# A later unit for the router's logits, and a row of scales in the softmax's buffer

## The chip, the cores and the metric

The kernel runs on one core of one Trainium2 chip. Its time is the device time of one execution in microseconds (us). The engines are TensorE (PE), VectorE (DVE), ScalarE (ACT), GpSimd (POOL), and SyncE (SP), which here only issues transfers.

## What is computed

Two gated residual blocks over x of 16 batches, 1024 tokens, width 512. First cross attention to 64 memory tokens per batch (4 query heads, one key/value head of 128), then a mixture of experts in which, for each group of 32 tokens, each of 128 expert slots takes the token with the highest logit.

```python
x = x + tanh(g_xattn) * xattn(layernorm(x), ctx, mask, ...)     # rmsnorm, q, k, rope, softmax over 64, values, out_w
x = x + tanh(g_ffn) * ffn(layernorm(x), Wc, bc, W1, b1, W2, b2)
# ffn, per group of 32 tokens:
logits = einsum('bntd,des->bntes', grouped, Wc) + bc + tie
perm = (logits == max(logits, over the 32 tokens))
inner = relu(einsum(perm-gathered tokens, W1) + b1)
out = scatter(einsum(inner, W2) + b2, perm)
```

The router's logits are taken of layernorm(x1), x1 being the output of the first block. The kernel gets them as a product of Wc with x and another with the attention's values, and multiplies every token's column by the token's scale r = 1/sqrt(var + eps).

## The kernel before, in words

There are two stages, each written as five streams, one per engine, that meet only in semaphores. The order within a stream is written out by hand.

**Attention** (`attention`) runs over 32 units u of 512 tokens (`NU`, half a batch each) in a software pipeline: pass g of every engine's loop handles the softmax and values of unit g, the queries of unit g+1, and the splitting of x for unit g+2. TensorE's pass (`tensor`): transposes of the logits (L906), three of four query products of the next unit (L879), `part_of_x` of the next unit (L939), transposes of the softmax's result `pr` (`probs_T`, L913), the fourth query product, `part_of_values` (L952), the attention's values (L926) with the attention's logits between them (L894).

**The router's logits** pass through the ring `lx` of `LX_RING` places. ScalarE copies the part from x there (`part_of_x`, L595), VectorE adds the part from the values (`both_parts`, L726), GpSimd multiplies by the row of scales `rrow` (`scaled_logits`, L535), and SP stores the result to `lg_scratch` (L355). ScalarE's copy of unit u waits until the store of unit u - LX_RING has landed. In ScalarE's stream the copies `probs` (pTh, L589) stand behind it; VectorE's pTl (L705) follows them, and part_of_values needs both.

**The row of scales.** GpSimd's `row_scale(u)` (L505 to L511) makes r of unit u at the end of pass u+1. SP's `logits_out(u)` stores it to `r_scratch` (L351), waits until it landed, loads it back broadcast to 128 partitions as `rrow` (L353), waits for the product, and stores the logits (L355). SP calls it for unit u-1 within its turn for unit u, between the store of the unit's second half of x1 (L427) and the reload of that place with x of unit u+4 (L433). GpSimd takes the product of unit g-2 in pass g right behind the softmax's two products `pr` (L543), and then come the rotation (L528, L529), the split `xTl` (L515), `norm_scale` and `row_scale`.

**Between the stages.** SP ends the stage with `logits_out` of unit 31, waits for the last stores, and loads W1's second ring piece, which lies in the last quarter of `xin` (L458).

**Experts** (`experts`) runs over the 16 batches: gather (L1380) and first layer (L1407) in eight pieces of W1, the scatter of the batch before (L1446), second layer (L1431), routing of the next batch. W1's pieces 2, 4 and 5 are resident; piece 3, the middle piece, is loaded to `xin` (`load_middle`, L1185), the four end pieces run through a ring of two (`load_end`, L1177). GpSimd scales the tokens of the next batch in place (`Router.normed`, L182; tiles 0 to 3 early, 4 to 7 late) and issues the accumulating stores of the batch before (`add_to_out`, L1236), the last four of them once the last moved piece of W2 has landed. The first gather of the second half needs tile 7. The middle piece's quarters wait for the last four of those stores.

Of the kernel before, what the change touches and what calls it, by code (L numbers as in the profile page):

```python
# [17 lines left out]
P = 128  # L18
# [6 lines left out]
NT = T // P  # L25
# [13 lines left out]
LX_RING = 3  # L39
# [29 lines left out]
def build(nc, x, xT_in, ctx_in, ctxT_in, mask, gx_in, gf_in, rms, q_w, kv_w, out_w, out_wT, Wc, bc, W1, b1, W2, b2,  # L69
# [7 lines left out]
    with top:  # L77
# [29 lines left out]
        attn = attention(nc, top, ps, ident, small, gate_x, gate_f, xin, xT, consts, const_loads, kept, kept_loads, d_kept,  # L107
                         ring, ring_loads, d_ring, route, m_b2s, x, xT_in, ctx_in, ctxT_in, mask, gx_in, gf_in, rms, q_w, kv_w, out_w, out_wT, Wc,
                         ident_in, cos_in, sin_in, b2, kr_dram, vc_dram, out)
        ffn = experts(nc, top, ps, kept, d_kept, consts, ident, gate_f, xin, ring, d_ring, route, m_b2s, W1, W2, out)  # L110
# [105 lines left out]
def attention(nc, top, ps, ident, small, gate_x, gate_f, xin, xT, consts, const_loads, kept, kept_loads, d_kept,  # L216
# [17 lines left out]
    with st:  # L234
# [19 lines left out]
        rrow = sb("rrow", [P, HT])  # L254
# [50 lines left out]
        mean_of = qs[:, 0, 0:P]  # L305
        gts = sb("gts", [P, 2])
# [38 lines left out]

        def sync(e):
            def logits_out(u):

                i, h = u // 2, u % 2
                e.wait_ge(route.m_r.sem, route.m_r.at(i, h))  # L350
                e.dma_start(route.r_dram[i, h], route.r[:, i, h * TH:(h + 1) * TH]).then_inc(d_r.sem, 16)  # L351
                e.wait_ge(d_r.sem, d_r.at(u))
                e.dma_start(rrow[:], route.r_dram[i, h].rearrange("p t -> (p t)").partition_broadcast(P)).then_inc(d_rr.sem, 16)  # L353
                e.wait_ge(m_lsr.sem, m_lsr.at(u))
                e.dma_start(route.lg_dram[i, h], lx[:, u % LX_RING, :]).then_inc(d_lgs[u % LX_RING].sem, 16)  # L355

# [52 lines left out]
            for u in range(NU):  # L409
# [7 lines left out]
                if u == NU - 1:  # L417
                    for n in range(2):
                        e.wait_ge(d_lgs[n].sem, d_lgs[n].at((NU - 3 - n) // LX_RING))
                    e.wait_ge(m_L.sem, m_L.at(NU - 1))  # L420
                    for h in range(2):
                        route.load_logits(e, 0, h)
                k = u % RING
                for h in range(2):
                    v = slice(2 * h, 2 * h + 2)
                    e.wait_ge(m_rs.sem, m_rs.at(u, 2 * h + 1))
                    e.dma_start(unit_tokens(x1_dram, u)[:, v], xin[:, k, v]).then_inc(d_o[k].sem, 16)  # L427
                    if h and u:
                        logits_out(u - 1)
                    if u + RING < NU:  # L430
                        e.wait_ge(d_o[k].sem, d_o[k].at(u // RING, h))
                        e.wait_ge(m_s1.sem, m_s1.at(u, 2 * h + 1))
                        e.dma_start(xin[:, k, v], unit_tokens(x, u + RING)[:, v]).then_inc(d_x[k][h].sem, 16)  # L433
                    if h == 0 and unit(u + 3):
                        e.wait_ge(m_lo.sem, m_lo.at(u + 2, C - 1))
                        e.dma_start(xT[:], turned_x(u + 3)).then_inc(d_xT.sem, 16)
# [15 lines left out]
            logits_out(NU - 1)  # L452
            for k in (2, 3):
                e.wait_ge(d_o[k].sem, d_o[k].at(NU // RING - 1, 1))
            for k in range(LX_RING):
                e.wait_ge(d_lgs[k].sem, d_lgs[k].at((NU - 1 - k) // LX_RING))
            for c in range(QUARTERS):
                e.dma_start(quarter(ring[1], c), quarter(ring_loads[1], c)).then_inc(d_ring[1][c].sem, 16)  # L458

        def gpsimd(e):  # L460
# [70 lines left out]
            def scaled_logits(u):  # L531
                o = lx[:, u % LX_RING, :].rearrange("p (t s) -> p t s", s=P)
                e.wait_ge(m_ls.sem, m_ls.at(u))
                e.wait_ge(d_rr.sem, d_rr.at(u))
                e.tensor_tensor(o, o, rrow[:].rearrange("p (s t) -> p t s", t=TH), ALU.mult).then_inc(m_lsr.sem, 1)  # L535

            for g in range(-1, NU):
                if unit(g):
                    for tp in range(2):
                        e.wait_ge(m_rc.sem, m_rc.at(g, tp))  # L540
                        if g:
                            e.wait_ge(m_PT.sem, m_PT.at(g - 1, tp))
                        e.tensor_tensor(heads(pr_[:, tp, :]), heads(lg[:, tp, :]),  # L543
                                        rc[:, tp, :].unsqueeze(2).broadcast_to([P, 8, S]), ALU.mult).then_inc(m_pr.sem, 1)
                if unit(g - 2):
                    scaled_logits(g - 2)
# [16 lines left out]
                if unit(g - 1):  # L563
                    row_scale(g - 1)
                if g >= NU - 2:
# [479 lines left out]
        return Stage(sync, gpsimd, scalar, vector, tensor)  # L1045


def experts(nc, top, ps, kept, d_kept, consts, ident, gate_f, xin, ring, d_ring, route, m_b2s, w1_dram, w2_dram, out):
# [7 lines left out]
    with st:  # L1056
# [114 lines left out]
        def sync(e):  # L1171
# [33 lines left out]
            for i in range(B + 1):  # L1205
                if live(i):
                    if i != 1:
                        for c in range(QUARTERS):
                            load_middle(i, c)
                    for k, c in ((0, 0), (0, 1), (1, 0), (1, 1), (1, 2), (1, 3), (0, 2), (0, 3)):  # L1210
# [21 lines left out]
        def gpsimd(e):  # L1232
# [5 lines left out]
            for i in range(B):  # L1238
# [3 lines left out]
                for t in range(NT):  # L1242
                    if live(i - 1):
                        if t == NY:
                            e.wait_ge(d_room[W2_MOVED[2]].sem, d_room[W2_MOVED[2]].at(i, QUARTERS - 1))
                        add_to_out(i - 1, t)
                if live(i + 1):
                    for t in range(NY, NT):
                        route.normed(e, i + 1, t)
# [283 lines left out]
```

## Time and profile before

| what | value |
|---|---|
| median of 3 runs | 1894.57 us (1873.33 to 1895.8) |
| profiled execution | 1886.3 us, span 1884.5 us |
| TensorE busy | 1668.2 us, 89% |
| VectorE busy | 1292.8 us, 69% |
| GpSimd busy | 854.0 us, 45% |
| ScalarE busy | 724.3 us, 38% |
| mean granted clock of TensorE | 0.959 of full |

The span is from the first to the last instruction, and the profiled execution's own time is 1.8 us longer. Busy time is counted per engine and says nothing on what it waits for; for that there are the list of waits, the chain of waits (the work that ended last, followed back from release to release) and the timeline. The attention stage lasts to about 1000 us of the span.

### The profile page before, as it was taken

Reading aid. Unit: us, or ns where it says so; the run is one execution under the profiler, and the core shown is the slowest. Engines: PE = TensorE matmul, PEld = TensorE weight load, DVE = VectorE, ACT = ScalarE, POOL = GpSimd, SP = SyncE. Lnnn points to the kernel's source line nnn. Section 1 sums busy time; section 2 is a strip of 40 time slices with the busy share of each in tenths; the row PEclk is TensorE's granted clock in tenths of the full one; section 3 lists DMA queues with packets and bytes.
Section 4 is the critical chain, followed back from the end, with each engine's and each line's share of the span. In section 5 each row is a group of like instructions: output and inputs, shape, how many; then the busy total and the mean of one; then the engine's idle time right before and its main releaser. Section 6 shows DMA issues by size and latency. Waiting matters only on the chain.

```text
span 1884.5 us, 51838 instructions
## 1 busy us (share of the span) xinstructions
PE 1668.2 (89%) x22488; PEld 1167.2 (62%) x22488; DVE 1292.8 (69%) x1886; ACT 724.3 (38%) x965; POOL 854.0 (45%) x1016
## 2 busy tenths in 40 slices
PE   7898989889889889898985799989998999999895
PEld 4676667667667666676764455666665555556662
DVE  6676766766767666676663477777777777777676
ACT  3532222322222222222211455555555555555452
POOL 3466666766766766667661122212222222221212
PEclk9999999999999999999987899999999999999998
DMA  7524434435444354344443488777777888887676
GB/s 264 159 102 147 161 116 135 166 111 178 137 134 140 114 168 138 128 140 132 150 145 112 153 220 220 218 205 220 206 208 213 216 225 225 218 216 210 190 187 165
DMA packets 180882, 324.81 MB, mean 172 GB/s; under 512 B 23344, under 2 KB 33328, under 8 KB 179248
## 3 DMA queue, kind: packets, MB, share of 16 engines
q1 hardware_dynamic: 135728, 239.68, 38.7%
q0 software_dynamic: 17280, 31.46, 10.0%
q10 hardware_dynamic: 27648, 50.34, 8.3%
q8 instruction: 179, 2.93, 0.7%
q14 instruction: 47, 0.39, 0.1%
HBM read 242.71 MB, written 78.71 MB: 171 GB/s over the span
## 4 chain that ended last, share of the span: by engine, by line
POOL 32%; PE 29%; DMA 23%; issue 9%; DVE 3%; ACT 2%; ACTq 1%; SPq 1%; POOLq 0%; DVEq 0%
PE ps L1407 13%; POOL xTl L515 8%; DMA gat<-in_W 8%; PE ps L1380 7%; DMA r_scratch<-r_all 7%; DMA rrow<-r_scratch 6%; POOL qc L528 4%; POOL qc L529 4%; POOL xin L182 3%; POOL lx L535 3%; POOL vw L552 2%; POOL r_all L507 2%; PE ps L1431 2%; POOL r L489 2%; POOL r L497 2%
## 5 line engine op out<-in xcount | busy, mean ns | idle before, releaser
L182 POOL TENSOR_SCALAR xin<-xin,r_all,nb_all 128x512 f32<-128x512 f32 x128 | 115.3, 1178 | 400.5 <-DMA xin<-out 400.4
L1312 DVE STREAM_TRANSPOSE res<-res 128x2048 f32<-128x2048 f32 x128 | 292.1, 2295 | 0.1
L1264 ACT ACTIVATE gat<-ps 128x1536 f32<-128x1536 f32 (+1 forms) x128 | 171.3, 1344 | 249.1 <-PE ps L1380 249.1
L879 PE MATMUL ps<-xTh,qh 128*128 128x512 f32 x512 | 209.3, 409 | 5.3 <-DVE qs L694 1.4
L1328 DVE COPY res<-ps 128x1024 f32<-128x1024 f32 x128 | 156.7, 1225 | 82.3 <-PE ps L1431 82.3
L1236 POOL DMA_DIRECT2D out<-xin x120 | 105.9, 1166 | 232.7 <-DMA gat<-in_W 151.6
L1380 PE MATMUL ps<-sel,xin 32*128 32x128 f32 x4096 | 161.5, 294 | 52.0 <-POOL xin L182 27.4
L879 PE MATMUL ps<-xTh,ql 128*128 128x512 f32 x512 | 200.3, 391 | 0.0
L879 PE MATMUL ps<-xTl,qh 128*128 128x512 f32 x512 | 199.9, 390 | 0.0
L1318 DVE COPY gat<-ps 128x512 f32<-128x512 f32 (+1 forms) x128 | 103.9, 813 | 118.6 <-PE ps L1380 117.6
L926 PE MATMUL ps<-vw,pTh 128*128 128x512 f32 x512 | 180.2, 436 | 0.0
L1380 PEld LDWEIGHTS ps<-sel,xin 32*128 32x128 f32 x4096 | 137.9, 197 | 66.4 <-issue 41.9
L1274 ACT ACTIVATE res<-ps 128x1024 f32<-128x1024 f32 x128 | 131.1, 1024 | 92.7 <-PE ps L1431 92.7
L515 POOL TENSOR_TENSOR xTl<-xT,xTh 128x512 fp32r<-128x512 f32 x128 | 160.4, 1283 | 12.3 <-ACT xTh L578 12.3
L595 ACT ACTIVATE lx<-ps 128x512 f32<-128x512 f32 x32 | 19.1, 597 | 348.1 <-DMA lg_scratch<-lx 323.4
L709 DVE TENSOR_TENSOR xin<-ps,xin 128x512 f32<-128x512 f32 x128 | 88.2, 689 | 88.1 <-PE ps L926 88.1
L926 PEld LDWEIGHTS ps<-vw,pTh 128*128 128x128 f32 x512 | 106.1, 212 | 49.6 <-issue 25.2
L528 POOL TENSOR_TENSOR qc<-qc,qs 128x512 f32<-128x512 f32 x64 | 82.4, 1287 | 113.8 <-DVE qs L694 113.8
L705 DVE TENSOR_TENSOR pTl<-ps,pTh 128x512 fp32r<-128x512 f32 x64 | 41.3, 686 | 134.4 <-ACT pTh L589 134.4
L535 POOL TENSOR_TENSOR lx<-lx,rrow 128x512 f32<-128x512 f32 x32 | 49.3, 1540 | 180.7 <-DMA rrow<-r_scratch 180.7
L1407 PE MATMUL ps<-gat,xin 128*64 128x64 f32 x3072 | 102.7, 225 | 18.3 <-DMA xin<-in_W 17.1
L879 PEld LDWEIGHTS ps<-xTh,qh 128*128 128x128 f32 x512 | 96.2, 188 | 36.0 <-DVE qs L694 18.8
(156 smaller groups left out, 3399.2 us busy)
## 6 DMA issues: line engine op xcount, KB each, us to landing
gat<-in_W ACTq DMA_DIRECT2D x192, 256.0 KB, 5.6
xT<-in_xT SPq DMA_DIRECT2D x32, 1024.0 KB, 6.6
xin<-in_x SPq DMA_DIRECT2D x64, 512.0 KB, 3.8
out<-xin SPq DMA_DIRECT2D x64, 512.0 KB, 2.9
xin<-out SPq DMA_DIRECT2D x128, 256.0 KB, 4.4
xin<-in_W SPq DMA_DIRECT2D x128, 256.0 KB, 3.6
out<-xin POOLq DMA_DIRECT2D x120, 256.0 KB, 8.6
xT<-in_W SPq DMA_DIRECT2D x68, 256.0 KB, 4.4
```

Of the source, the lines that this page charges most:

```text
L182: e.tensor_scalar(self.xn[:, t, :], self.xn[:, t, :], self.r[:, i, t:t + 1], self.nb[:, i, t:t + 1], ALU.mult, ALU.add).then_inc(self.m_xn ...
L515: e.tensor_tensor(xTl[:, c, :], xT[:, c, :], xTh[:, c, :].bitcast(F32), ALU.subtract).then_inc(m_lo.sem, 1)
L528: e.tensor_tensor(qc[:, 2 * p, :], qc[:, 2 * p, :], qs[:, 2 * p + 1, :], ALU.subtract).then_inc(m_rot.sem, 1)
L879: last = e.matmul(ps[:, 2 + n % 2, :], a[:, c, n * DH:(n + 1) * DH], b[:, c, :], start=(k == 0), stop=(k == len(parts) - 1))
L926: last = e.matmul(ps[:, 5 + t % 2, :], a[:, t // 2, column:column + P], vw[:, u // 2 % 2, k, p, :], start=(m == 0), stop=(m == len(parts) ...
L1236: e.dma_start(batch(out, b, t, 1)[:, 0], tile_of(t), accum_op=ALU.add).then_inc(d_ys[t].sem, 16)
L1264: e.activation(o, v, ACT.Copy).then_inc(m_gaA.sem, 1)
L1274: e.activation(o, v, ACT.Copy).then_inc(m_evA.sem, 1)
L1312: e.transpose(v, v).then_inc(m_tr.sem, 1)
L1328: e.tensor_copy(o, v).then_inc(m_evV.sem, 1)
L1380: last = e.matmul(ps[:, front(n) + g, t * E:(t + 1) * E], xn[r, h * TH + t, c * P:(c + 1) * P], sel[r, h * TH + t, :], start=True, stop=True)
L1407: last = e.matmul(ps[a * 64:(a + 1) * 64, q // 8, q % 8 * 64:(q % 8 + 1) * 64], first(i, p)[:, (e0 % 64) * F:(e0 % 64 + 2) * F], gat[:, c ...
```

## The change

The ring `lx` gets a fourth place, and the whole path of a unit's logits behind the row of scales comes a unit later on SP: in its turn for unit u SP stores and reloads the scales of unit u-2 (`scales_back`, ahead of the unit's stores, behind a wait for the unit's transposes of the softmax) and stores the logits of unit u-2 (`logits_out`). `rrow` is no longer a buffer of its own but the first half of `pr_`. GpSimd takes the product at the end of its pass. The logits of unit 31 go out from the experts' stream, behind the loads of W1's middle piece (`last_logits`); W1's second ring piece is loaded behind `scales_back` of unit 30. In the experts, GpSimd's four later norms alternate with the four later stores, a norm first.

```diff
-LX_RING = 3
+LX_RING = 4
...
-        rrow = sb("rrow", [P, HT])
...
+        rrow = pr_[:, 0, :]
...
+        def scales_back(e, u, g):
+
+            i, h = u // 2, u % 2
+            e.wait_ge(route.m_r.sem, route.m_r.at(i, h))
+            e.dma_start(route.r_dram[i, h], route.r[:, i, h * TH:(h + 1) * TH]).then_inc(d_r.sem, 16)
+            e.wait_ge(d_r.sem, d_r.at(u))
+            e.wait_ge(m_PT.sem, m_PT.at(g, 1))
+            e.dma_start(rrow, route.r_dram[i, h].rearrange("p t -> (p t)").partition_broadcast(P)).then_inc(d_rr.sem, 16)
+
+        def logits_out(e, u):
+            e.wait_ge(m_lsr.sem, m_lsr.at(u))
+            e.dma_start(route.lg_dram[u // 2, u % 2], lx[:, u % LX_RING, :]).then_inc(d_lgs[u % LX_RING].sem, 16)
+
+        def last_logits(e):
+
+            scales_back(e, NU - 1, NU - 1)
+            logits_out(e, NU - 1)
+            for k in range(LX_RING):
+                e.wait_ge(d_lgs[k].sem, d_lgs[k].at((NU - 1 - k) // LX_RING))
+
         def sync(e):
-            def logits_out(u):
...
                 if u == NU - 1:
                     for n in range(2):
-                        e.wait_ge(d_lgs[n].sem, d_lgs[n].at((NU - 3 - n) // LX_RING))
+                        e.wait_ge(d_lgs[n].sem, d_lgs[n].at((NU - 4 - n) // LX_RING))
...
+                if u >= 2:
+                    scales_back(e, u - 2, u)
...
-                    if h and u:
-                        logits_out(u - 1)
+                    if h and u >= 2:
+                        logits_out(e, u - 2)
...
-            logits_out(NU - 1)
             for k in (2, 3):
                 e.wait_ge(d_o[k].sem, d_o[k].at(NU // RING - 1, 1))
-            for k in range(LX_RING):
-                e.wait_ge(d_lgs[k].sem, d_lgs[k].at((NU - 1 - k) // LX_RING))
+            scales_back(e, NU - 2, NU - 1)
+            e.wait_ge(m_s1.sem, m_s1.at(NU - 1, TH - 1))
             for c in range(QUARTERS):
                 e.dma_start(quarter(ring[1], c), quarter(ring_loads[1], c)).then_inc(d_ring[1][c].sem, 16)
+            logits_out(e, NU - 2)
...
                         if g:
                             e.wait_ge(m_PT.sem, m_PT.at(g - 1, tp))
+                        if g >= 3 and tp == 0:
+                            e.wait_ge(m_lsr.sem, m_lsr.at(g - 3))
...
-                if unit(g - 2):
-                    scaled_logits(g - 2)
                 if unit(g + 1):
                     rotated(g + 1, 0)
...
                 if unit(g - 1):
                     row_scale(g - 1)
+                if unit(g - 2):
+                    scaled_logits(g - 2)
...
                     if i != 1:
                         for c in range(QUARTERS):
                             load_middle(i, c)
+                    if i == 0:
+                        last_logits(e)
...
-                for t in range(NT):
+                if live(i - 1):
+                    for t in range(NY):
+                        add_to_out(i - 1, t)
+                    e.wait_ge(d_room[W2_MOVED[2]].sem, d_room[W2_MOVED[2]].at(i, QUARTERS - 1))
+                for t in range(NY, NT):
+                    if live(i + 1):
+                        route.normed(e, i + 1, t)
                     if live(i - 1):
-                        if t == NY:
-                            e.wait_ge(d_room[W2_MOVED[2]].sem, d_room[W2_MOVED[2]].at(i, QUARTERS - 1))
                         add_to_out(i - 1, t)
-                if live(i + 1):
-                    for t in range(NY, NT):
-                        route.normed(e, i + 1, t)
```

## Rows read from the trace of the kernel before

**Rows 1.** Page of the profile, part 4: the chain that ended last, by line.

```profile
PE ps L1407 13%; POOL xTl L515 8%; DMA gat<-in_W 8%; PE ps L1380 7%; DMA r_scratch<-r_all 7%; DMA rrow<-r_scratch 6%; POOL qc L528 4%; POOL qc L529 4%; POOL xin L182 3%; POOL lx L535 3%; POOL vw L552 2%; POOL r_all L507 2%; PE ps L1431 2%; POOL r L489 2%; POOL r L497 2%
```

**Rows 2.** Chain in order of time, one unit: start us, us, what.

```profile
517.61 3.40 DMA r_scratch<-r_all
...
521.02 3.15 DMA rrow<-r_scratch
...
524.31 1.54 POOL lx L535
```

**Rows 3.** Waits, 120 to 960 us: who for whom: us in total, times, longest.

```profile
ACT lx L595 <- DMA lg_scratch<-lx: 312.5, 28, 13.4
...
POOL lx L535 <- DMA rrow<-r_scratch: 152.6, 29, 6.7
...
PE ps L952 <- DVE pTl L705: 74.8, 27, 4.4
```

**Rows 4.** Timeline: start us, us, engine, line, operation [idle before <-releaser].

```profile
528.26 0.60 ACT L595 ACTIVATE lx<-ps 128x512 f32<-128x512 f32 x1 [10.51 <-DMA lg_scratch<-lx]
...
530.92 0.47 PE L952 MATMUL ps<-pTh,voh 128*128 128x512 f32 x1 [2.48 <-DVE pTl L705]
```

**Rows 5.** Timeline of TensorE: transposes of the softmax in four of the units.

```profile
127.71 1.03 PE L913 MATMUL ps<-ident,pr 128*128 128x128 f32 x8
...
152.73 1.03 PE L913 MATMUL ps<-ident,pr 128*128 128x128 f32 x8
...
933.54 1.03 PE L913 MATMUL ps<-ident,pr 128*128 128x128 f32 x8
...
958.89 1.03 PE L913 MATMUL ps<-ident,pr 128*128 128x128 f32 x8
```

**Rows 6.** Windows: stretch, us, busy (x) PE PEld DVE ACT POOL, PEclk, DMA, GB/s.

```profile
400.00:700.00 300.00, 272.97 (x1281) 205.35 (x1280) 203.35 (x432) 76.32 (x135) 202.03 (x242) 0.97 0.44 145
...
532.50:536.80 4.30, 4.30 (x13) 3.13 (x11) 1.39 (x2) 0.42 (x1) 4.27 (x4) 0.61 0.00 0
...
933.54:958.89 25.35, 25.09 (x124) 18.83 (x122) 18.72 (x40) 7.09 (x13) 19.44 (x24) 1.00 0.32 104
```

**Rows 7.** Timeline of GpSimd in the unit of 933.54 to 958.89 us.

```profile
952.35 0.20 POOL L511 TENSOR_TENSOR nb_all<-mv,ns 128x4 f32<-128x4 f32 x1
952.50 2.05 POOL L543 TENSOR_TENSOR pr<-lg,rc 128x512 f32<-128x512 f32 x2
```

**Rows 8.** DMA issues, 120 to 960 us: times, KB each, median us to landing.

```profile
rrow<-r_scratch SPq DMA_DIRECT2D x29, 256.0 KB, 3.2
lg_scratch<-lx SPq DMA_DIRECT2D x29, 256.0 KB, 2.2
...
r_scratch<-r_all SPq DMA_DIRECT2D x29, 2.0 KB, 4.3
```

**Rows 9.** Waits of SP's queue, 120 to 960 us.

```profile
SPq L427 <- DVE xin L709: 301.1, 58, 11.0
```

**Rows 10.** Chain in order of time, from attention to experts.

```profile
1001.54 4.55 DMA r_scratch<-r_all
1006.11 4.43 DMA rrow<-r_scratch
...
1023.28 3.22 DMA xin<-in_W
```

**Rows 11.** Timeline of TensorE there: first layer's second product, seventh product.

```profile
1026.55 3.69 PE L1407 MATMUL ps<-gat,xin 128*64 128x64 f32 x64 [17.11 <-DMA xin<-in_W]
...
1044.30 1.97 PE L1407 MATMUL ps<-gat,xin 128*64 128x64 f32 x62
```

**Rows 12.** Waits, 1080 to 1800 us.

```profile
PE ps L1380 <- POOL xin L182: 26.1, 15, 4.4
```

**Rows 13.** Timeline of GpSimd in one batch: later stores, then later norms.

```profile
1380.71 3.54 POOL L1236 DMA_DIRECT2D out<-xin  x4 [11.75 <-DMA gat<-in_W]
1382.92 4.33 POOL L182 TENSOR_SCALAR xin<-xin,r_all,nb_all 128x512 f32<-128x512 f32 x4
```

More of the change, by code:

```diff
@@ L106, in build @@
         ring_loads = [W1[0], W1[1]]
-        attn = attention(nc, top, ps, ident, small, gate_x, gate_f, xin, xT, consts, const_loads, kept, kept_loads, d_kept,
+        attn, last_logits = attention(nc, top, ps, ident, small, gate_x, gate_f, xin, xT, consts, const_loads, kept, kept_loads, d_kept,
                          ring, ring_loads, d_ring, route, m_b2s, x, xT_in, ctx_in, ctxT_in, mask, gx_in, gf_in, rms, q_w, kv_w, out_w, out_wT, Wc,
                          ident_in, cos_in, sin_in, b2, kr_dram, vc_dram, out)
-        ffn = experts(nc, top, ps, kept, d_kept, consts, ident, gate_f, xin, ring, d_ring, route, m_b2s, W1, W2, out)
+        ffn = experts(nc, top, ps, kept, d_kept, consts, ident, gate_f, xin, ring, d_ring, route, m_b2s, last_logits, W1, W2, out)
         with nc.Block() as blk:
@@ L344, in attention @@
         turned_x = lambda u: xT_in[u // 2].rearrange("(c p) t -> p c t", p=P)[:, :, u % 2 * HT:(u % 2 + 1) * HT]
-        def sync(e):
-            def logits_out(u):
[L349 to L355, printed above, removed]
+        def scales_back(e, u, g):
[13 more added lines that the diff above has]
+                e.wait_ge(d_lgs[k].sem, d_lgs[k].at((NU - 1 - k) // LX_RING))
+        def sync(e):
             e.dma_start(rs1[:], rms).then_inc(d_rs.sem, 16)
@@ L534, in scaled_logits @@
                 e.wait_ge(d_rr.sem, d_rr.at(u))
-                e.tensor_tensor(o, o, rrow[:].rearrange("p (s t) -> p t s", t=TH), ALU.mult).then_inc(m_lsr.sem, 1)
+                e.tensor_tensor(o, o, rrow.rearrange("p (s t) -> p t s", t=TH), ALU.mult).then_inc(m_lsr.sem, 1)
             for g in range(-1, NU):
@@ L1043, in tensor, with experts @@
             e.wait_ge(m_rs.sem, m_rs.at(NU - 1, TH - 1))
-        return Stage(sync, gpsimd, scalar, vector, tensor)
-def experts(nc, top, ps, kept, d_kept, consts, ident, gate_f, xin, ring, d_ring, route, m_b2s, w1_dram, w2_dram, out):
+        return Stage(sync, gpsimd, scalar, vector, tensor), last_logits
+def experts(nc, top, ps, kept, d_kept, consts, ident, gate_f, xin, ring, d_ring, route, m_b2s, last_logits, w1_dram, w2_dram, out):
     st = ExitStack()
```

## The prediction

> **What bounds the kernel now.** I read the chain of waits by line first. Besides TensorE's product lines it holds three steps that compute nothing: the store of r_scratch, the load of rrow from it, and GpSimd's idle time before the product with it [rows 1]. The chain in order of time shows them one after the other in a unit of the attention stage: 3.40 us for the store, 3.15 us for the load, then the product of 1.54 us [rows 2]. The list of waits of 120 to 960 us says who pays. ScalarE's copy of a unit's x part (part_of_x) waits 28 times, 312.5 us in all, for a store of logits, because the ring lx has three places; GpSimd waits 152.6 us in 29 units for rrow. TensorE itself waits 74.8 us in 27 units, always before part_of_values, for pTl [rows 3]. The timeline links them: the copy starts 10.51 us late, the pTh copies stand behind it on ScalarE, pTl behind these, and TensorE idles 2.48 us [rows 4].
>
> What a unit would take without this is in the trace. From one unit's first transpose of the softmax to the next it was 25.02 us while the ring was still filling, and 25.35 us once late in the stage, where no idle time stood before part_of_values. Between them, 152.73 to 933.54 us, lie 27 units, and with the last one 28: (958.89 - 152.73)/28 = 28.79 us each [rows 5]. The idle time is not the whole of the difference. Behind the gap the clock falls to one of its two levels: 0.61 granted over 4.3 us, so mostly 1.2 GHz, against 1.00 in the undisturbed unit [rows 6].
>
> **The change part by part, attention.** (1) LX_RING 4: part_of_x(g+1) waits for the store of unit g-3, no longer g-2. (2) The product with rrow moves from behind the softmax's products to the end of GpSimd's pass. In the undisturbed unit GpSimd ended row_scale at 952.35 + 0.20 = 952.55 us and the two softmax products, 2.05 us, followed at once [rows 7]. With 1.54 us put ahead of them they end at 956.1 us; TensorE wants them at 958.89 us [rows 5]. Slack 2.8 us, so the move costs nothing; without that slack each us late costs one per unit. (3) The logits' store is issued at 952.55 + 1.54 = 954.1 us and lands in 2.2 us [rows 8], at 956.3 us, 2.6 us before the next x part is ready to be copied. (4) rrow now lies in the softmax's own buffer and must wait for its transposes, which in that unit end at about 933.54 + 1.03 = 934.6 us [rows 5]. SP, which has done the previous unit's second reload by then, needs 4.3 + 3.2 us for store and load [rows 8]: rrow is there by 942 us, needed at 952.6 us, slack 10 us. Added waits: one of SP on the transposes, one of GpSimd on its own last product (free, that engine runs in order). Behind SP's wait are the unit's two stores, its reload of x and that of xT. They wait for the second attention sum anyway: SP stands idle for these sums 301.1 us in 58 stores, 5 us each [rows 9], and that idle time covers what is put ahead. No instruction or byte is added; eight wait instructions or so move.
>
> So TensorE becomes the bound of the stage. I take 25.2 us a unit, between the two undisturbed ones: 28 x (28.79 - 25.2) = 100.5 us. The unit behind 958.89 us has a small gap and slow clock too, and gives about 3 us. Bounds: 28 x (28.79 - 25.35) = 96 us and 28 x (28.79 - 25.02) = 106 us. **Attention: -103 us.**
>
> Against this stands a reading by busy share. TensorE was busy 272.97 of 300 us in mid stage [rows 6]: 27 us idle in 10.4 units, 2.6 us each, or 28 x 2.6 = 73 us. The Trainium skill (Perfetto Trace Analysis, Identifying the Most-Contended Engine) says matmul busy time is no good measure of distance from the limit; the trace agrees, as matmuls at 1.2 GHz count as busy. By busy share the whole sum would be -90 us, by the undisturbed units it is the one below.
>
> **Transition.** TensorE stands 17.11 us before the second product with W1's ring piece, up to 1026.55 us [rows 10, 11]. SP issues that piece only at 1023.28 us, behind both detours of unit 31: store, rrow, product, store of logits [rows 10]. After the change only the last stores' landing (to about 1006 us, as the 4.55 us row), one r_scratch store and the issue of rrow lie ahead: issue at about 1008 us, landed like before with 3.22 us plus the rrow load in front of it, 1012 us. Gain 14.5 us. Part is given back. The middle piece follows unit 30's logits (1012 + 1.5 us) in two rounds of 3.2 us and some issue, lands by 1021 us, in time for its product at about 1020 us. Then SP does unit 31's detour from 1018 us: 4.3 + 3.2 + 1.5 + 2.2 us, to about 1029.5 us, and only then loads W1's two end pieces. Their products begin 17.75 us behind the second [rows 11], so at 1029.8 us; their quarters land from 1033.5 to 1038 us. That costs 6.5 us. **Transition: -8 us**; bounds -14 (nothing given back) and -2.
>
> SP's detour is priced by its rows. [...] The 4.3 us row of a 2 KB store speaks for queueing behind other traffic, so I keep the rows.
>
> **Experts.** GpSimd today issues four adds and then scales tiles 4 to 7: 3.54 us of issue and norms to 1387.25 us from 1380.71 us [rows 13], so 0.88 us per add and about 0.8 us per norm. TensorE waits for the last norm 26.1 us in 15 batches [rows 12]. With one norm ahead of each add, the last norm has three adds before it instead of four: up to 0.88 us earlier, where GpSimd and not the load of the tile is late. The last add comes later by up to 3 us; behind it is the reload of W1's middle piece, which is needed far later, and on SP the ring pieces. I take -0.4 us x 14 = **-6 us**; bounds -12 (0.88 in every batch) and +8 (half a us lost in each through SP's queue).
>
> Sum: -103 - 8 - 6 = -117 us on the profiled execution's 1886.3 us: 1769 us. The median is 8 us above that execution. What varies between runs are mostly transfers on the chain, and the new unit has slack against them; I take 1771 us.
>
> **Rivals.** A: the ring's wait stays in part. The store may land later than 2.2 us, or SP be late for it. The slack is 2.6 us and another us or so behind it before TensorE feels it; stores that land 2 us beyond that would cost 1.5 us per unit with the slow clock, 42 us: 1813 us. For it: the r_scratch row of 4.3 us for 2 KB. Against: the logits' own row. Chance 0.11. B, **slower**: rrow is late, now that its load hangs on the transposes and on SP's queue, and the softmax's products stand behind the product with it. It decides from 942 + 10 + 2.8 = about 955 us on, 13 us later than forecast; each us more costs 28. To be over 2% slower than now a unit must take 30.2 us, so rrow must come 5 us later still: 1935 us. Against: the same two transfers end 7 us after their start today. Chance 0.02. C: the pacing engine is another, GpSimd with its chain from the rotation through xTl and norms to the products; then the ring's gain is lost and the time stays near 1885 us. For it: GpSimd leads the chain's lines [rows 1]. Against: it sat idle for rrow 5 us a unit [rows 3]. Chance 0.04.
>
> **Numbers.** My forecast holds 0.83: its own range is 1748 to 1800 us (bounds of the three terms, and some 10 us between runs). To leave out no more than 2 in 10, I go to 1808 us for the mild part of A. A measurement tells 2% from no change: under 1857 us is faster. A and the forecast lie there, with 0.01 of A beyond: 0.93. C: 0.05 with that. B: 0.02.
>
> **What would show it.** Right: ScalarE's wait on the logits' store nearly gone, units of 25.0 to 25.4 us, clock 1.00 in the stage, TensorE's gap before part_of_values gone; one gap of 2 to 4 us at W1's second piece and a new one at its end pieces; the last add of a batch 3 us later. Wrong: softmax's transposes waiting for their products (B, C), or the ring's wait over 4 us a unit (A). The forecast fails if an engine other than TensorE ends the unit.

## The result, and the profile after

| | before | after |
|---|---|---|
| median, us | 1886.67 (1873.33 to 1895.8, 4 runs) | 1772.31 (1766.51 to 1775.78, 4 runs) |
| profiled execution, its span | 1886.3, 1884.5 | 1775.6, 1773.8 |
| mean granted clock | 0.959 | 0.977 |

Ratio 0.940, interval [0.932, 0.947]: 6% faster. The forecast was 1771 us. The time between two marks on TensorE's timeline splits the profiled pair. A unit is the time from the first transpose of the softmax in the 3rd unit to that in the 31st, over 28. The tail goes from there to the experts' first gather, the transition from there to batch 1's first gather, the experts from there to the first product of the last batch's scatter.

| stretch, us | before | after | change | forecast |
|---|---|---|---|---|
| 28 units | 28 x 28.79 | 28 x 24.99 | -106.6 | -100.5 |
| tail | 42.3 | 38.6 | -3.7 | -3 |
| transition | 73.1 | 68.9 | -4.2 | -8 |
| experts | 784.7 | 790.1 | +5.4 | -6 |

**Attention.** TensorE's transposes of the softmax in three units of the changed kernel, the 3rd, the 31st and the last, which answer to [rows 5] (columns as there):

```profile
151.01 1.03 PE L927 MATMUL ps<-ident,pr 128*128 128x128 f32 x8
...
850.60 1.03 PE L927 MATMUL ps<-ident,pr 128*128 128x128 f32 x8
871.63 2.12 PE L927 MATMUL ps<-ident,pr 128*128 128x128 f32 x8 [7.31 <-POOL pr L557]
```

The 28 units between the first two take 699.6 us, 24.99 us each. The list of waits, 120 to 850 us, answers to [rows 3]:

```profile
ACT lx L609 <- PE ps L953: 210.5, 28, 8.0
...
ACT lx L609 <- DMA lg_scratch<-lx: 8.6, 1, 8.6
...
POOL pr L557 <- POOL lx L547: 4.7, 28, 0.2
```

ScalarE now waits for TensorE's part_of_x and not for a store; one wait that the profile puts down to a store is left, and it is hardly longer than the waits for TensorE. No row with TensorE waiting for pTl is left. GpSimd does not wait for rrow in any of these units: no such row is in the list either. In mid stage the windows view (columns as [rows 6]) has 298.62 of 300 us busy, at clock 1.00:

```profile
400.00:700.00 300.00, 298.62 (x1467) 227.16 (x1466) 233.36 (x494) 93.82 (x156) 236.16 (x277) 1.00 0.51 162
```

GpSimd's timeline in a unit, which answers to [rows 7]:

```profile
544.39 1.55 POOL L547 TENSOR_TENSOR lx<-lx,pr 128x512 f32<-128x512 f32 x1
...
546.11 2.05 POOL L557 TENSOR_TENSOR pr<-lg,rc 128x512 f32<-128x512 f32 x2 [0.17 <-POOL lx L547]
```

Its softmax products end at 548.16 us and TensorE's transposes of them begin at 550.77 us, 2.6 us later; in the next unit it was 3.3 us. The forecast had 2.8 us.

The last unit shows what the moved product costs when rrow is late. TensorE stands 7.31 us before the transposes above at 871.63 us. In the kernel before it stood 4.51 us at the same place, when VectorE's part of the softmax was late there:

```profile
980.79 2.17 PE L913 MATMUL ps<-ident,pr 128*128 128x128 f32 x8 [4.51 <-POOL pr L543]
```

So the late rrow costs 2.8 us of the 7.31. The chain of waits there is

```profile
855.15 7.12 DMA r_scratch<-r_all
862.29 3.61 DMA pr<-r_scratch
```

SP issues the 2 KB store at 855.15 us, right behind nine loads for the next stage. The store takes 7.12 us beside them, rrow lands at 865.9 us, and the product and four norms (L182) stand ahead of the last softmax products. This is rival B, in one unit of 32.

**Transition.** TensorE's timeline, which answers to [rows 11]:

```profile
899.33 0.69 PE L1424 MATMUL ps<-gat,xin 128*64 128x64 f32 x16 [1.86 <-DMA xin<-in_W]
900.65 2.83 PE L1424 MATMUL ps<-gat,xin 128*64 128x64 f32 x48 [0.64 <-DMA xin<-in_W]
...
910.65 0.69 PE L1424 MATMUL ps<-gat,xin 128*64 128x64 f32 x16 [1.23 <-DMA xin<-in_W]
...
925.20 2.03 PE L1424 MATMUL ps<-gat,xin 128*64 128x64 f32 x32 [7.63 <-DMA xin<-in_W]
928.11 1.12 PE L1424 MATMUL ps<-gat,xin 128*64 128x64 f32 x16 [0.88 <-DMA xin<-in_W]
929.79 1.12 PE L1424 MATMUL ps<-gat,xin 128*64 128x64 f32 x16 [0.56 <-DMA xin<-in_W]
```

The 17.11 us are 2.50 us now, and a new idle time of 9.07 us stands at the end pieces. SP's timeline says why. The first end piece's loads are issued behind the store of unit 31's logits:

```profile
893.79 1.86 SPq L469 DMA_DIRECT2D xin<-in_W  x4
...
906.99 0.43 SPq L350 DMA_DIRECT2D r_scratch<-r_all  x1
...
915.51 0.32 SPq L357 DMA_DIRECT2D lg_scratch<-lx  x1
...
917.65 1.01 SPq L1191 DMA_DIRECT2D xT<-in_W  x2
```

**Experts.** Waits, 970 to 1690 us, which answer to [rows 12], and behind them, for the kernel before, two more rows of the view of [rows 12], 1080 to 1800 us:

```profile
PE ps L1397 <- issue: 17.2, 18, 1.7
...
PE ps L1424 <- issue: 11.7, 12, 3.0
...
PE ps L1397 <- POOL xin L182: 6.4, 11, 1.0
```

```profile
PE ps L1380 <- issue: 12.7, 12, 1.5
...
PE ps L1407 <- issue: 2.5, 4, 1.4
```

The wait for the norm fell from 26.1 to 6.4 us, and idle time of these two lines that the profile puts down to no wait ("issue") rose from 15.2 to 28.9 us. The experiments ask what that is, and whether the experts really lost 5 us.

### The profile page after: what moved, and what is told of

Same layout as the page of the kernel before. It is cut to its first block, busy times and chain, and to the rows that moved or that the text cites. A ratio compares the mean times of both kernels' runs of the same rounds, so it can differ in the third digit from the quotient of the medians.

```text
span 1773.8 us, 51856 instructions
## 1 busy us (share of the span) xinstructions
PE 1639.1 (92%) x22488; PEld 1152.8 (65%) x22488; DVE 1295.8 (73%) x1886; ACT 737.3 (42%) x965; POOL 856.1 (48%) x1016
## 4 chain that ended last, share of the span: by engine, by line
PE 60%; DMA 16%; DVE 11%; issue 5%; ACT 3%; POOL 2%; SPq 1%; ACTq 1%; POOLq 0%; DVEq 0%
PE ps L1424 13%; PE ps L893 10%; PE ps L940 10%; PE ps L1397 7%; PE ps L953 5%; DMA xin<-out 4%; DMA out<-xin 4%; DMA gat<-in_W 3%; PE ps L908 3%; PE ps L1448 3%; PE ps L966 3%; DVE mx L691 2%; PE ps L1463 2%; PE ps L927 2%; ACT lg L660 2%
## 5 line engine op out<-in xcount | busy, mean ns | idle before, releaser
L182 POOL TENSOR_SCALAR xin<-xin,r_all,nb_all 128x512 f32<-128x512 f32 x128 | 114.3, 897 | 533.0 <-DMA xin<-out 387.1
L1397 PEld LDWEIGHTS ps<-sel,xin 32*128 32x128 f32 x4096 | 133.9, 188 | 57.0 <-issue 30.1
L1252 POOL DMA_DIRECT2D out<-xin x120 | 121.4, 1086 | 94.6 <-DVE xin L1168 81.1
L940 PE MATMUL ps<-vw,pTh 128*128 128x512 f32 x512 | 164.6, 402 | 0.0
L707 DVE TENSOR_TENSOR qc<-ps,cos 128x512 f32<-128x512 f32 x128 | 86.8, 678 | 58.6 <-PE ps L893 58.3
L1424 PE MATMUL ps<-gat,xin 128*64 128x64 f32 x3072 | 108.0, 231 | 17.4 <-DMA xin<-in_W 12.8
L940 PEld LDWEIGHTS ps<-vw,pTh 128*128 128x128 f32 x512 | 94.3, 189 | 45.5 <-issue 25.2
L893 PEld LDWEIGHTS ps<-xTh,qh 128*128 128x128 f32 x512 | 96.2, 188 | 35.5 <-DVE qs L708 18.3
L1424 PEld LDWEIGHTS ps<-gat,xin 128*64 128x64 f32 x3072 | 101.0, 145 | 23.8 <-issue 14.2
```

Of the source, the lines that this page charges most:

```text
L182: e.tensor_scalar(self.xn[:, t, :], self.xn[:, t, :], self.r[:, i, t:t + 1], self.nb[:, i, t:t + 1], ALU.mult, ALU.add).then_inc(self.m_xn ...
L893: last = e.matmul(ps[:, 2 + n % 2, :], a[:, c, n * DH:(n + 1) * DH], b[:, c, :], start=(k == 0), stop=(k == len(parts) - 1))
L940: last = e.matmul(ps[:, 5 + t % 2, :], a[:, t // 2, column:column + P], vw[:, u // 2 % 2, k, p, :], start=(m == 0), stop=(m == len(parts) ...
L1252: e.dma_start(batch(out, b, t, 1)[:, 0], tile_of(t), accum_op=ALU.add).then_inc(d_ys[t].sem, 16)
L1397: last = e.matmul(ps[:, front(n) + g, t * E:(t + 1) * E], xn[r, h * TH + t, c * P:(c + 1) * P], sel[r, h * TH + t, :], start=True, stop=True)
L1424: last = e.matmul(ps[a * 64:(a + 1) * 64, q // 8, q % 8 * 64:(q % 8 + 1) * 64], first(i, p)[:, (e0 % 64) * F:(e0 % 64 + 2) * F], gat[:, c ...
```

## The experiments

All medians stand beside a run of the kernel before on the same chip (1873 to 1887 us). Stretches are cut as in the table above.

**1. Was it the ring, or the two transfers ahead of the logits' store?** The kernel before, ring of three, without store and reload of the scales.

```diff
             def logits_out(u):
-                e.wait_ge(route.m_r.sem, ...)
-                e.dma_start(route.r_dram[i, h], ...)
-                e.wait_ge(d_r.sem, d_r.at(u))
-                e.dma_start(rrow[:], ...)
                 e.wait_ge(m_lsr.sem, m_lsr.at(u))
...
+            e.memset(rrow[:], 1.0).then_inc(d_rr.sem, 16)
...
-                e.wait_ge(d_rr.sem, d_rr.at(u))
+                e.wait_ge(d_rr.sem, d_rr.at(0))
```

The product is made with a row of ones, so this kernel leaves the scales out of the router's logits.

> The kernel before, its ring of three places and its order kept, with only the detour of the scales left out: no store to r_scratch, no load of rrow; the product is made with a row of ones, so the router's logits go out unscaled. Theory 1 (the two transfers hold the product back, hence the logits' store, hence ScalarE's copy and TensorE): softmax transposes 25.0 us apart at clock 1.00 with three places already, ScalarE's wait on lg_scratch under 20 us in all, and with the transition's detours gone too about 1760 us. Rival (three places are too few for this order whatever the transfers do): units stay above 27 us and ScalarE goes on waiting several us per unit for lg_scratch, time above 1830 us.

Measured: 1771.39 us (1767.76 to 1775.01), ratio 0.944 [0.936, 0.952]; unit 24.995 us. The waits of 120 to 850 us:

```profile
ACT lx L592 <- PE ps L936: 218.7, 29, 8.1
```

No wait on a store is in the list. So three places are enough where SP does not hold the logits back for the detour: the ring was too small only for the 6.5 us of [rows 2]. A fourth place with the path a unit later, and three places with the shorter path, buy the same unit, and both stop at it: TensorE is the bound at 25.0 us. A fourth place alone, with the detour and the product where they were, was not run, so its share is not shown. Both kernels also free GpSimd of its wait for rrow. That this wait cost TensorE nothing by itself is read from the list before, where TensorE never waits for the softmax's products from 120 to 960 us; no run tests it alone. The later product with a ring of three wasn't tried: at the end of pass g it would free the place that ScalarE wants within pass g.

**2. How much slack has GpSimd ahead of the transposes?** Idle operations of 1 us in each pass of 2 to 29, behind the product: two, then five.

```diff
                     scaled_logits(g - 2)
+                if 2 <= g < NU - 2:
+                    for k in range(2):      # 5 in the second kernel
+                        e.tensor_tensor(idle[:, k, :], eps_l[:, 0:TH], nhalf[:, 0:TH], ALU.pow)
```

> The changed kernel with two idle pow instructions of 1.02 us each at the end of GpSimd's passes 2 to 29, ahead of the softmax's products. Theory (GpSimd has 2.6 to 3.3 us of slack before the transposes): no change, within 4 us of 1772 us, units still 25.0 us, transposes not waiting. Rival (GpSimd's chain is as long as TensorE's and only looks hidden): each us shows, 28 x 2 = 56 us more.

> The changed kernel with five idle pow instructions of 1.02 us each at the same place, 5.1 us in a pass. Theory (slack 2.6 to 3.3 us): the excess of 1.8 to 2.5 us shows in every one of 28 units, 60 us, with slow clock behind the gap up to 100 us: 1830 to 1870 us, TensorE waiting for the softmax's product in every unit. Rival (GpSimd has far more slack, nothing there could have turned into a bound): under 1790 us.

Measured: with two 1769.80 us (1761.95 to 1777.66), unit 24.996 us, no change. With five 1804.86 us (1804.61 to 1805.12), unit 26.39 us, less than expected. GpSimd's and then TensorE's timeline with five:

```profile
568.71 4.92 POOL L582 TENSOR_TENSOR idle<-eps_layer,nhalf 128x4 f32<-128x4 f32 x5
```

```profile
574.70 0.66 PE L931 MATMUL ps<-ident,pr 128*128 128x128 f32 x4 [0.95 <-POOL pr L558]
575.70 0.65 PE L931 MATMUL ps<-ident,pr 128*128 128x128 f32 x4 [0.34 <-POOL pr L558]
```

The transposes come in two groups of four, and the first needs only the first of the two softmax products, which ends 1.02 us before the second. So the slack is about 2.6 + 1.0 = 3.6 us, and 4.92 - 3.6 = 1.3 us is about what a unit grew by (26.39 - 24.99 = 1.4). The two waits of a unit make 1.0 us of that on average (25.3 us in 26 units); the rest is counted as busy time. An extra loss through the clock, as in [rows 6], didn't come: TensorE's 52 waits for the softmax are of 1.0 us at most, and the windows view grants 1.00.

```profile
PE ps L931 <- POOL pr L558: 25.3, 52, 1.0
```

```profile
400.00:700.00 300.00, 287.58 (x1386) 214.46 (x1386) 222.93 (x471) 91.71 (x148) 277.29 (x323) 1.00 0.48 158
```

**3. Is the new end of the attention worth anything?** The changed kernel with the old order there.

```diff
             scales_back(e, NU - 2, NU - 1)
-            e.wait_ge(m_s1.sem, m_s1.at(NU - 1, TH - 1))
+            logits_out(e, NU - 2)
+            last_logits(e)
             ... # W1's second ring piece
-            logits_out(e, NU - 2)
... # in the experts, behind the loads of W1's middle piece
-                    if i == 0:
-                        last_logits(e)
```

> The changed kernel with the end of the attention stage in the old order: unit 30's and unit 31's detours and logits first, then W1's second ring piece; no detour behind the middle piece. Theory (the transition as changed wins 15 us at the second product and gives 11 to 13 back at the end pieces, 4 us net): 3 to 6 us slower than the changed kernel, about 1777 us; TensorE waits some 17 us for the ring piece and nothing for the end pieces. Rival (my forecast of 8 us net): 8 us or more slower.

Measured: 1773.96 us (1772.69 to 1775.98), transition 71.66 us against 68.91. Its waits, 860 to 960 us, have one long wait, and none at the end pieces:

```profile
PE ps L1422 <- DMA xin<-in_W: 16.1, 1, 16.1
```

Moving that wait to the end pieces saves 2.75 us in the trace. The medians, 1.6 to 4 us apart, can't confirm it.

**4. The experts' GpSimd order.** The changed kernel with four later stores first, then four norms, as before.

```diff
+                for t in range(NT):
+                    if live(i - 1):
+                        if t == NY:
+                            e.wait_ge(d_room[W2_MOVED[2]].sem, ...)
+                        add_to_out(i - 1, t)
+                if live(i + 1):
+                    for t in range(NY, NT):
+                        route.normed(e, i + 1, t)
```

> The changed kernel with the experts' order of before on GpSimd: four later stores, then four later norms. Theory F (the norms no longer hold TensorE up, but the time is taken again by idle time marked issue, which the old wait had hidden): the same time as the changed kernel within 4 us, waits for the last norm back at 20 to 26 us, issue idle lower by about the same. Rival (the alternation is worth the 18 us that the wait list shows): 1785 to 1790 us. Second rival (the alternation costs time through the later reload of the middle piece): 5 us or more faster than the changed kernel.

Measured: 1783.05 us (1778.1 to 1791.6), experts 803.6 us in the profiled execution, which was the slowest of the six. The unaltered kernel had 1772.31 us, and 1769.97 us (1766.61 to 1783.81) in a later series: the old order costs 11 to 13 us. The kernel of experiment 3, which alternates and ran in the same series as this one, lies with all its six runs (1772.69 to 1775.98 us) below all six here. Waits, 970 to 1690 us:

```profile
PE ps L1396 <- POOL xin L182: 35.2, 14, 4.3
...
PE ps L1396 <- issue: 12.2, 14, 1.8
```

My theory, no net gain because issue idle takes over what the norm gives back, fell. Against 6.4 and 28.9 us in the changed kernel, 28.8 us of waits for the norm went, and 16.7 us of issue idle came: more than half is given back, not all. Over the whole of the experts the issue idle is 13 to 15 us in the three profiles with the old order and 22 to 33 us in the nine with the alternation. The kernel before and experiment 1 have the old order too, and their experts took 784.7 and 790.1 us. So the 11 to 13 us are shown for this kernel; what the order was worth in the kernel before is not.

**5. What is "issue"?** If the gaps sit at places of the instruction stream, eight more transposes ahead of the experts must move each gap by eight matmuls.

```diff
             e.wait_ge(m_pl.sem, m_pl.at(NU - 1, 1))
+            for k in range(8):
+                e.transpose(ps[:, 1, ...], route.selT[0][:, ...], ident[:])
             route.chosen_T(e, 0, 1)
```

> The changed kernel with eight transposes more (eight weight loads and eight matmuls, on a bank written anyway) just ahead of the last chosen_T between the stages. Theory F (the idle time marked issue lies where a block of TensorE's instruction stream ends): every such gap moves by eight matmuls, so that the groups behind it grow from x6, x9 and x39 to x14, x17 and x47, at unchanged cost. Rival (the gaps belong to operations, their operands or their waits): they stay before x6, x9 and x39. Time within 5 us of the changed kernel in both cases.

Measured: 1771.96 us (1771.59 to 1772.33). Three gaps of one batch on TensorE's timeline, in the changed kernel and in this one:

```profile
1127.07 0.50 PE L1397 MATMUL ps<-sel,xin 32*128 32x128 f32 x6 [1.06 <-issue]
...
1132.20 1.38 PE L1424 MATMUL ps<-gat,kept 128*64 128x64 f32 x39 [0.61 <-issue]
...
1142.06 0.59 PE L1397 MATMUL ps<-sel,xin 32*128 32x128 f32 x9 [1.36 <-issue]
```

```profile
1123.22 0.72 PE L1401 MATMUL ps<-sel,xin 32*128 32x128 f32 x14 [1.01 <-issue]
...
1128.13 1.62 PE L1428 MATMUL ps<-gat,kept 128*64 128x64 f32 x47 [0.40 <-issue]
...
1137.59 0.82 PE L1401 MATMUL ps<-sel,xin 32*128 32x128 f32 x17 [0.96 <-issue]
```

The groups left behind the gap grow from 6, 39 and 9 matmuls to 14, 47 and 17: eight each. It is so in the whole trace: counted in matmuls from the first gather, 30 of its 32 issue gaps lie exactly eight ahead of a place where one of the other thirteen traces has one. Those places are 126.3 matmuls apart, or a multiple of it, which with one weight load for each matmul makes 253 instructions. (One more gap, ahead of batch 0's second layer, stands at the same place in every trace and is not of this kind.) The gap belongs to a place in the stream and not to a step of the algorithm. The Trainium skill (Runtime: NRT & Kernel Launch, Instruction fetch mechanics) says that an engine's instruction memory is refilled in blocks of 256 instructions and that crossing a block is "mostly hidden". Gaps at fixed places of the stream, 253 instructions and some waits apart, agree with the blocks. "Mostly hidden" holds by count, as about 100 of the stage's 135 places show no gap; but the others cost 29 us in 30 gaps from 970 to 1690 us.

**6. Does the issue idle come from the data traffic?** The changed kernel with every weight load of the experts at a quarter of its columns, so that it computes with partly stale weights.

```diff
-                e.dma_start(quarter(ring[k], c), quarter(w1_dram[...], c))...
+                e.dma_start(quarter(ring[k], c)[:, 0:P], quarter(w1_dram[...], c)[:, 0:P])...
... # W1's middle piece and W2's moved ones in the same way
```

> The changed kernel with every load of expert weights in the experts' stage (moved pieces of W2, end pieces and middle piece of W1) cut to a quarter of its bytes, same number of transfers and instructions; the experts compute with partly stale weights. Theory F (TensorE's idle time marked issue, 29 us in the experts, always at nearly the same place of the instruction stream, is late instruction blocks behind the data traffic): issue idle in the experts falls to 10 us or less, time 1735 to 1750 us with the waits for weights gone. Rival (these gaps are fixed costs of the stream or lost records and have nothing to do with traffic): they stay at about 29 us and only the 10 us of waits for weights between the stages go, 1760 us or more.

Measured: 1694.98 us (1694.77 to 1695.18), 40 us below the range expected; experts 720.8 us, with no issue idle and no wait for a norm. The windows view of the experts, changed kernel first:

```profile
970.00:1690.00 720.00, 664.80 (x15589) 425.80 (x15584) 538.83 (x441) 391.19 (x442) 181.10 (x222) 0.99 0.79 213
```

```profile
970.00:1620.00 650.00, 628.51 (x15384) 403.00 (x15382) 529.18 (x436) 391.66 (x442) 184.26 (x224) 1.00 0.61 137
```

TensorE's busy share goes from 0.92 to 0.97 as the DMA engines' goes from 0.79 to 0.61. The gaps at the ends of instruction blocks are there only while the data transfers are dense. Of the 69 us that the stage is shorter by, 32 us are issue idle and 8 us waits for the norm. Another 31 us are busy time, 692 us against 723 us for the same products, and no run explains them.

The traces also hold the start and duration of every packet that the DMA engines moved, and these show the instructions themselves. In the experts of the changed kernel 135 packets of 16 KB pass the queue marked "instruction", as many as there are blocks of 126.3 matmuls. All 35 issue gaps of the stage end 1.25 to 1.61 us behind the landing of one of them, and of the 40 other gaps only one does; the landings are 5.7 us apart in the median. With the weight loads in full a packet starts 2.8 us (median) behind the end of the block before, with a quarter of them 0.7 us; once started it takes 1.0 and 1.1 us. So it is the start of the fetch that comes late beside dense data, not its transfer.

**7. Take back what the transition gives back.** First `last_logits` is split: the scales go behind the fourth of the end pieces' quarters, the store of logits ahead of the last. Then SP also issues the 2 KB store of the scales a turn earlier.

```diff
                     for k, c in (...):
+                        if i == 0 and (k, c) == (1, 2):
+                            last_logits[0](e)     # scales_back(31)
+                        if i == 0 and (k, c) == (0, 3):
+                            last_logits[1](e)     # logits_out(31)
                         load_end(i, k, c)
# second kernel, in SP's turn for unit u
                     if h and u >= 2:
                         logits_out(e, u - 2)
+                    if h and 1 <= u < NU - 1:
+                        scales_out(e, u - 1)      # no longer in scales_back
```

> The changed kernel with unit 31's detour spread between the loads of W1's end pieces: scales back after the fourth of the eight quarters, logits out before the last. Theory (the end pieces are late by the whole detour, 11 to 13 us): TensorE waits 3 us instead of 9 at the end pieces, 8 to 10 us faster than the changed kernel, about 1763 us. Rival (something else, as the loads of x for the next batch or the moved W2 pieces, comes late next): within 3 us of the changed kernel.

> The one before, and SP stores the scales of unit u-1 already in its turn u, behind the logits' store, so that turn u+1 only loads them. Theory (in unit 31 the softmax's product stands 2.9 us behind its reciprocal, as GpSimd waits 5.9 us for scales whose store took 7.1 us behind the kept and ring loads; elsewhere the detour has slack): 2 to 3 us faster than the split alone, units still 25.0 us. Rival (the load of the scales is late by the same traffic and nothing is won): within 1 us of it.

Measured: 1767.12 us (1762.9 to 1772.23), transition 62.63 us, less of a gain than expected; with the early store 1763.83 us (1756.46 to 1765.68), transition 62.23 us, tail 35.48 us against 38.05 with the split alone. Waits of the first, 860 to 960 us:

```profile
PE ps L1427 <- DMA xin<-in_W: 3.6, 2, 2.2
...
PE ps L1427 <- DMA xT<-in_W: 0.9, 1, 0.9
```

12.8 us of waits for W1 became 4.5. Is the sum of it in the time? The changed kernel and the one with the early store, both again, side by side:

> The changed kernel unaltered, in more rounds beside the others: about 1772 us. Its experts' part, 790 us in the first profile, should on this theory lie near 784 us on average (forecast -6 us against the old order, which gave 785 to 804 us), since e3 with the old order was 1783 us; rival: 790 us is its true size and the alternation brought nothing.

> The split with the early store of the scales again, beside the changed kernel in the same rounds: 8 to 10 us faster than that (6 us from the end pieces, 2.6 us from unit 31). Rival: under 4 us faster, the rest being spread between executions.

Measured: 1769.97 us (1766.61 to 1783.81), ratio 0.947 [0.943, 0.952], and 1766.34 us (1753.86 to 1779.66), ratio 0.944 [0.939, 0.949]. The stretches agree with the first runs (transition 64.5 against 68.2 us, tail 35.5 against 39.5 us), 7.7 us together, but the medians are 3.6 us apart, as the rival said, and the intervals overlap. It is the fastest kernel found, and that it beats the changed one is not shown.

**8. All four norms ahead of the later stores.** The kernel of 7 with the early store, to take the last 7 us of norm waits.

```diff
                 for t in range(NY, NT):
                     if live(i + 1):
                         route.normed(e, i + 1, t)
+                for t in range(NY, NT):
                     if live(i - 1):
                         add_to_out(i - 1, t)
```

> The one before with GpSimd's four later norms all ahead of the four later stores. Theory (the last norm has nothing ahead of it but norms, TensorE's wait of 7 us for it goes to 3 or less, but idle time marked issue takes most of it back): within 3 us of the one before. Rival 1 (norms are what is left to win): 5 us faster. Rival 2 (the stores, up to 3 us later, make the middle piece late): 5 us or more slower, with TensorE waiting for xin of W1 inside the batches.

Measured: 1788.15 us (1784.7 to 1792.85), 22 us slower, experts 806.9 us. Waits, 970 to 1690 us, of this kernel and then of the one it was made from:

```profile
DVE sel L191 <- DMA sel<-lg_scratch: 55.1, 11, 9.1
...
PE ps L1474 <- DVE xin L1176: 20.2, 8, 5.9
...
PE ps L1435 <- DMA xin<-in_W: 2.3, 2, 1.3
```

```profile
DVE sel L191 <- DMA sel<-lg_scratch: 14.4, 9, 6.3
...
PE ps L1473 <- DVE xin L1176: 2.5, 2, 2.3
```

My theory fell, and the second rival came by a way of its own. The wait for the norm is gone, and a dearer one took its place. W1's middle piece, for which SP waits on the later stores (85.0 us against 54.2 in its queue's list), costs TensorE only 2.3 us itself. But SP issues the load of the next logits behind it; VectorE waits 41 us more for them and finishes the outputs late, for which TensorE's scatter waits 18 us more. Alternating norm and store lies between two cliffs, 11 to 13 us on the one side and 22 us on the other.

## Why the prediction was right, and where a term was mis-sized

**Attention, right.** The chain as told was the cause: logits' store, part_of_x, pTh, pTl, part_of_values. Experiment 1 takes away only its head and gets all of the gain. The unit came out at 24.99 us, not the 25.2 that I took, at the lower undisturbed unit of [rows 5]: -106.6 us against -100.5, beyond the lower bound by less than 1 us. The reading by busy share, 73 us, fell. It missed 34 us, and most of that is the slow clock, which counts as busy: from 120 to 960 us the kernel before was granted 0.97, so about 25 us (an estimate) went there, in 16 stretches like the one of [rows 6], not one in every unit.

**The slacks, right in size, one read too strictly.** GpSimd 2.8 us forecast, 2.6 to 3.3 measured. But "without that slack each us late costs one" begins only at 3.6 us, as the first group of transposes needs one product alone (experiment 2). rrow was never late in the steady units, so the slack of 10 us was not used up. In unit 31, where the forecast looked only at SP's part, it came after 7.1 + 3.6 us of transfers and cost TensorE 2.8 us (7.31 against 4.51 before). The early store took 2.6 to 4.0 us of the tail away (experiment 7), which is that.

**Transition, gain right, give-back mis-sized.** From the first gather to the second product it took 10.16 us against 25.41 before: -15.25 us, forecast -14.5. Given back: second to seventh product 25.87 us against 17.75, +8.1; seventh product to the end of the eighth 9.1 against 3.9, +5.2; 13.3 in all where the term had 6.5; the rest of the stretch gave 2.3 more. The detour of unit 31 cost what I had priced it at, 10.7 us from 906.99 to 917.65 us against 11.2. What I priced too low are W1's quarters: I took the 3.22 us of [rows 10], which is the first and shortest of them. In the changed kernel those of the ring piece landed 5.5 to 6.7 us behind their issue, those of the middle piece 2.9 to 5.5 us and those of the end pieces 2.9 to 6.9 us. So the detour began 13.2 us behind the ring piece's issue and not 10, and the waits stand in the middle piece (1.23 us) and, in three, at the end pieces. -4.2 us lies within the bounds -14 and -2.

**Experts, the mechanism right, its size hidden in the pair.** "The last norm has three adds before it instead of four" is what happened: on GpSimd's timeline the last norm ends 5.8 us behind the wait ahead of it, in the batch from 1268.45 us, against 6.5 us in [rows 13]. But 26.1 us of waits became 6.4, where 6 of 26 was forecast. That is 1.3 us in each of 15 batches, more than the 0.88 us that I had as the most; where the rest comes from stays open. What failed is the silent premise that idle time taken from one wait stays away: 14 us of it came back as issue idle. The +5.4 us of the profiled pair is no measure of the change. Nine profiles with the alternating order have 777 to 790 us (mean 784), three with the old order 785 to 804 (mean 793), and by the medians of experiment 4 the order is worth 11 to 13 us, at the bound of -12.

The table's sum, -109 us, with 1.6 us outside its stretches, is the difference of the two profiled executions, 110.7 us. The forecast had 117: the terms' errors, -7 for attention with its tail, +4 and +11, cancel in part. That the median is so near the 1771 us has a share of luck, as it lies 3 us below its profiled execution.

The rivals: A (the ring's wait stays) did not come: one wait of 8.6 us in the stage. C (another engine paces) did not: five idle operations on GpSimd were needed to bring it about. B came in the last unit alone. Its price was summed wrongly: a unit of 30.2 us, or rrow 5 us later still, gives 1771 + 28 x 5 = 1911 us, 1% slower than before and not over 2%; 1935 us needs units of 31.1 us.

## What to carry over

When a buffer's ring makes an engine wait, look at what the freeing transfer itself waits for: a longer ring with a later path and a shorter path to the store were worth the same here, and neither more than the distance to the next engine's bound, which undisturbed units of the same trace show. Price the transfers behind a bulk load by rows that also stand behind one, and a group of loads by its slowest row, and ask of every reordered store which queue's next load waits for it. A wait that is taken away can come back as idle time at block ends of the instruction stream as long as the stage's data traffic is dense, so judge by the length of the stretch, over several executions.

## What the runs showed of the hardware

- Issue idle of TensorE in the experts, 13 to 33 us an execution, lies at fixed places of the instruction stream, 126.3 matmuls apart or a multiple of it, and shifts with it by exactly the eight matmuls added; with the stage's traffic at 137 GB/s and not 213 there was none.
- Each of these gaps in the changed kernel ended 1.25 to 1.61 us behind the landing of a 16 KB instruction packet. The packets took 1.0 us each, but started 2.8 us behind the end of the block before, against 0.7 us at 137 GB/s (medians).
- The 2 KB store of the scales took 1.4 us at 892.00 us of the changed kernel, 3.5 us in the median of its attention stage, and 7.12 us beside the loads of the last unit.
- In the kernel before, gaps of mostly 2 to 3.5 us, one in each unit, went with 16 stretches at 1.2 GHz from 120 to 960 us [rows 4, 6]; gaps of at most 1.0 us, 52 of them, left the granted clock at 1.00 (experiment 2).
- The experts' stretch of one and the same kernel took 790.1 us in one profiled execution and 782.5 us in another; the attention's 28 units agree within 0.2 us in these two.
